# One order for r's sums at every place below slot 896, and no product at place 12

## What is computed

```
mixed = tanh(x @ W_in.T + b_in + cond)
h1 = GRU(mixed); h2 = GRU(h1)            # 1024 steps each, one after another
   # step: r = sigmoid(xr + hr); z = sigmoid(xz + hz)
   #       n = tanh(xn + r * hn); h = (1 - z) * n + z * h
gate = sigmoid(cond @ W_gate.T + b_gate)
x = x + (gate * h2 + h2) @ W_out.T + b_out
shared = silu(x @ w1) * (x @ w3) @ w2                      # HS = 512
s = sigmoid(concat(x, cond) @ router_W); top 2 of 8 by s + router_bias
routed = sum over the chosen experts of weight * gelu(x @ W1e) @ W2e
out = x + (shared + routed) / 3
```

## Time and profile before

| | |
|---|---|
| time, median of 3 runs | 2154.06 us (2152.3 to 2155.34) |
| the profiled execution: time | 2159.05 us |
| its span, first to last instruction | 2157.3 us |
| its granted TensorE clock | 0.999 |
| PE, DVE, ACT, POOL busy | 95%, 84%, 52%, 26% of the span |
| instructions | 162,384, of them 70,040 matmuls and 70,040 weight loads |

### The profile page before, as it was taken

One profiled execution on the slowest core, in us unless ns is written; L12 is line 12 of the kernel. 1 busy time (PEld: TensorE's weight loads), 2 busy tenths in 40 slices (PEclk: granted clock), 3 DMA queues, 4 the chain that ended last, 5 costly groups with the idle time before them and its releaser, 6 DMA issues.

```text
span 2157.3 us, 162384 instructions
## 1 busy us (share of the span) xinstructions
PE 2057.2 (95%) x70040; PEld 1503.5 (70%) x70040; DVE 1818.3 (84%) x11337; ACT 1128.8 (52%) x6471; POOL 563.1 (26%) x2540
## 2 busy tenths in 40 slices
PE   6999999999999999999999999999999999999997
PEld 4666667777677776777667777677767777777776
DVE  3888888888888888888888888898888888888885
ACT  2555555555555555555555555555555555555542
POOL 1222232222322223222232222322232222222220
PEclk9999999999999999999999999999999999999999
DMA  5000000000000000000000000000000000000000
GB/s 222 5 5 5 4 5 5 5 5 5 10 5 5 5 5 10 5 5 5 10 5 5 5 5 10 5 5 5 5 10 5 5 5 10 5 5 9 5 5 9
DMA packets 7184, 24.32 MB, mean 11 GB/s; under 512 B 1584, under 2 KB 3904, under 8 KB 6208
## 3 DMA queue, kind: packets, MB, share of 16 engines
q1 hardware_dynamic: 6464, 13.93, 1.7%
HBM read 11.83 MB, written 2.10 MB: 6 GB/s over the span
## 4 chain that ended last, share of the span: by engine, by line
PE 72%; DVE 18%; ACT 7%; issue 2%; DMA 0%; SPq 0%; DVEq 0%
PE bank L336 34%; PE bank L328 20%; PE bank L268 14%; DVE bank L407 6%; DVE cells L427 5%; ACT factors L489 4%; DVE z_pre L408 3%; PE bank L309 3%; DVE r_pre L398 3%; ACT cells L493 2%; DVE bank L416 0%; PE bank L275 0%; DMA x_t<-in_x_t 0%; DVE n_second L383 0%; DVE x L707 0%
## 5 line engine op out<-in xcount | busy, mean ns | idle before, releaser
L336 PE MATMUL bank<-w_h,cells 128*22 128x128 f32 (+4 forms) x32768 | 1379.0, 281 | 20.3 <-DVE cells L427 11.8
L336 PEld LDWEIGHTS bank<-w_h,cells 128*22 128x22 f32 (+4 forms) x32768 | 867.5, 111 | 128.3 <-DVE cells L427 82.1
L328 PEld LDWEIGHTS bank<-w_h,cells 128*2 128x2 f32 (+15 forms) x28112 | 527.8, 113 | 480.4 <-DVE cells L427 452.2
L534 POOL TENSOR_SCALAR cells<-cells 128x4 f32<-128x4 f32 x2048 | 466.7, 228 | 1498.8 <-DVE cells L427 1497.9
L328 PE MATMUL bank<-w_h,cells 128*2 128x64 f32 (+15 forms) x28112 | 784.0, 225 | 65.5 <-DVE cells L427 53.6
L483 ACT ACTIVATE n_second<-r_pre 128x4 f32<-128x4 f32 x2048 | 426.4, 208 | 517.9 <-DVE r_pre L398 475.5
L489 ACT ACTIVATE factors<-z_pre 128x4 f32<-128x4 f32 x2048 | 429.4, 210 | 475.2 <-DVE z_pre L408 428.8
L427 DVE TENSOR_TENSOR_SCAN cells<-factors,cells 128x18 f32<-128x18 f32 x2048 | 396.5, 194 | 215.8 <-ACT cells L493 140.6
L407 DVE STREAM_TRANSPOSE bank<-bank 128x64 f32<-128x64 f32 x2048 | 522.4, 255 | 57.3 <-PE bank L336 34.8
L398 DVE STREAM_TRANSPOSE r_pre<-bank 128x64 f32<-128x64 f32 x2048 | 483.8, 236 | 33.3 <-PE bank L328 21.9
L408 DVE STREAM_TRANSPOSE z_pre<-bank 128x64 f32<-128x64 f32 x2048 | 428.9, 209 | 0.0
(11 more groups left out here) (93 smaller groups left out, 616.4 us busy)
## 6 DMA issues: line engine op xcount, KB each, us to landing
x_t<-in_x_t SPq DMA_DIRECT2D x4, 512.0 KB, 6.8
w_1e<-in_w_1e SPq DMA_DIRECT2D x1, 2048.0 KB
w_2e<-in_w_2e SPq DMA_DIRECT2D x1, 2048.0 KB
w_x<-in_w_x SPq DMA_DIRECT2D x2, 768.0 KB, 8.0
w_h<-in_w_h SPq DMA_DIRECT2D x2, 768.0 KB, 9.4
w<-in_w SPq DMA_DIRECT2D x3, 512.0 KB
out_y<-y SPq DMA_DIRECT2D x6, 256.0 KB, 3.3
w_in<-in_w_in SPq DMA_DIRECT2D x1, 256.0 KB, 2.7
```

The costliest lines, as they stand in the source:

```text
L328: mm = pe.matmul(r_sums[l][p][32 * g:32 * g + B * (j + 1)], state_tile(l, j, kt), w_h[l][:, kt, g, 2 * U:], start=False, stop=False, tile_ ...
L336: mm = pe.matmul(sums[l][p][32 * g:32 * g + B * (j + 1), 0:width], state_tile(l, j, kt), w_h[l][:, kt, g, 0:width], start=False, stop=Fals ...
L534: pool.tensor_scalar(cell_part(step_rows(l, j), 3), cell_part(step_rows(l, j), 1), 0.5, None, ALU.mult)\
```

## The change

Below slot 896 `r_first` is true at all places; from 896 on it is false at 0, 4, 8 and 12 as before. In windows of 128 steps PE may have no mixture product at place 12; the planner then puts the same products into later half slots.

```
 def r_first(l, t):
     s = t + LAG * l
-    return s % CH not in ((0, 4, 8, 12) if s >= SHORT else (4, 12))
+    return s < SHORT or s % CH not in (0, 4, 8, 12)
...
     def busy(self, engine, h):
         j, part = (h // 2 + self.begin) % CH, h % 2
         if engine == "pe":
-            return j in projection_pieces(part ^ 1) or part == 1 and (self.sparse or self.window > 5 * CH and j % 8 != 6)
+            return j in projection_pieces(part ^ 1) or part == 1 and (self.sparse or self.window > 5 * CH and j % 8 != 6) or self.sparse and j == 12
```

## The result

The changed kernel takes 2213.1 us in the median (2208.66 to 2218.07, 5 runs) against 2155.34 us for the kernel before (2152.3 to 2160.56, 5 runs): the ratio is 1.0276, 95% interval 1.0247 to 1.0304. It is slower by 2.8%, 58 us. I had forecast slower by 0.5%, 2165.7 us, with 2185 as the upper end. The direction was right; the size was not, and the time lies outside the range, above my "stop after stop" rival of 2201 us.

A forecast was written before the change was run, and what follows sets the result against it. Bound by the dependency chain, with instruction supply close under it: +14.1 us in slots 152 to 895, −3.4 plus 0.9 put back in 19 to 151, total +11.6, so 2165.7 us median; range 2143 to 2185.

The forecast's parts named there:

- stop after stop: Rival: with no slack left, supply stops lock one after another; 3.705 us per block, 2201 us; chance 0.13.
- What bounds the kernel: Dependency chain of the two layers, with PE's instruction supply, blocks of 127.6 weight loads, as a second bound close under it.
- 84 with a stop: Slots 160 to 783, kernel before: of 214 blocks touching no one-bank slot, 84 counted as having a stop.
- Order of r: Places 4 and 12 below slot 896: r's transpose precedes the other layer's scan; 0.2 us less, if PE keeps up.
- priced 12 as ordinary: Place 12 without product: PE's work of 1.71 us fits the slot, so −0.20 us.
- Instructions: 3,552 more weight loads and matmuls each, 548 to 576 blocks; slots 160 to 783: 352.0 x 3.62 = 1274.2 us, +11.8.
- Every block is of the sort that took 3.62 us: Slots 160 to 783: one-bank slots' slack gone, every block takes the 3.62 us mean of blocks touching none.
- The correction that I made downward: Per-block time taken as 3.62 us, not the 3.64 seen in runs, since blocks would hold 3.46 against 3.50 us of path.
- Hidden: Rival: supply is hidden or waits no more often than now; only the path counts, −16 us, 2138 us; chance 0.22.
- It cancels: Rival: blocks of 3.585 us give no change in slots 160 to 783; 2152 to 2156 us; chance 0.15.
- The new wait is on DVE: Rival: r's early transpose blocks DVE, delaying layer 1's scan at place 4; path gives −12 rather than −16 us; no chance given.
- the signs that I had named: 576 packets, some 31,660 L328 loads, issue waits of 40 to 60 us, one-bank scan gap 0.83, mean slot about 2.04.

The follow-up runs named there:

- run with wide products: Changed kernel with each mixture product made by one matmul over the whole array in place of four over strips of 32; 2263.49 us, ratio 1.0473.
- before, one strip: Kernel before with only the first of the four strips of each mixture product, except in the last group; 2118.55 us, ratio 0.9783.
- four from slot 152: Kernel before with one-bank steps at places 0, 4, 8 and 12 from slot 152 on, at 4 and 12 before that; 2138.97 us, ratio 0.9934.
- four in all slots: Kernel before with one-bank steps at places 0, 4, 8 and 12 in all slots; 2151.03 us, ratio 0.9936.
- three: Kernel before with one more one-bank place below slot 896, 8 beside 4 and 12; 2155.87 us, ratio 0.995.
- changed, one strip: Changed kernel with only the first of the four strips of each mixture product, except in the last group; 2146.3 us, ratio 0.9914 to the kernel before.
- products alone: Kernel before with no product at place 12 in groups of 128 steps, order of r unchanged; 2160.3 us, ratio 1.0032.
- place 4 alone: Kernel before with the new order of r only at place 4; place 12 stays one-bank and keeps its product; 2182.64 us, ratio 1.0138.
- place 12 alone: Kernel before with the new order of r and no product only at place 12; place 4 stays one-bank below slot 896; 2187.21 us, ratio 1.0109.
- order alone: Kernel before with the new order of r at all places below slot 896, products still allowed at place 12; 2223.69 us, ratio 1.0285.
- before with padding: Kernel before with eight one-column matmuls into a spare PSUM column behind each one-bank step below slot 896; 2230.11 us, ratio 1.0316.
- before, flooded: Kernel before with eight more one-column matmuls of zero weights in each step of layer 0 below slot 896; 2506.97 us, ratio 1.1641.
- experiments 1 and 5: Kernel before with tiny matmuls added: behind each one-bank step (1; 2230.11 us), or in every layer 0 step (5; 2506.97 us), both below slot 896.

## Why the prediction was right in kind and wrong in size

The stretch of slots 160 to 783 in one profiled execution of each run, ordered by its weight loads. The run with wide products is left out, since its products hold PE longer.

| kernel | weight loads | blocks (/ 127.6) | us | us per block |
|---|---|---|---|---|
| before, one strip | 39,780 | 311.8 | 1233.9 | 3.96 |
| four from slot 152 | 39,920 | 312.9 | 1248.2 | 3.99 |
| four in all slots | 39,920 | 312.9 | 1248.8 | 3.99 |
| three | 41,173 | 322.7 | 1258.2 | 3.90 |
| changed, one strip | 42,277 | 331.3 | 1253.2 | 3.78 |
| products alone | 42,405 | 332.3 | 1261.4 | 3.80 |
| before | 42,422 | 332.5 | 1262.4 | 3.80 |
| place 4 alone | 43,668 | 342.2 | 1279.0 | 3.74 |
| place 12 alone | 43,672 | 342.3 | 1294.1 | 3.78 |
| changed | 44,914 | 352.0 | 1311.6 | 3.73 |
| order alone | 44,916 | 352.0 | 1316.6 | 3.74 |
| before with padding | 44,914 | 352.0 | 1319.5 | 3.75 |
| before, flooded | 52,415 | 410.8 | 1516.8 | 3.69 |

At some 312 blocks the path sets the time (the waits for issue are 1.3 us in the second row); from 340 on the time per block stays near 3.7, and the time goes mostly by the count; the kernel before lies between, where both bounds count.

**What bounds the kernel: right.** That stops come a multiple of some 128 loads apart, that the two bounds lie close together, and that the second is the supply of instructions holds in every run that bears on it. In the prediction, "84 with a stop" of the dense blocks is more than the 72 waits of the whole stretch in the table, which leaves out the shortest; counted down to 0.1 us, the same trace has 88.

**Order of r: right for the slot, wrong for its neighbour.** The 0.2 us were won at places 4 and 12. I had a cost for place 4 only, where a product stands beside the projection, and priced 12 as ordinary. In fact the projection alone makes PE late with the first step behind it, and the slots at places 5 and 13 take 0.14 us more. The term was −0.27 us for 16 slots and −0.40 in the early slots; where no stop falls it measured −0.14 and −0.23. The early stretch so won less than I had credited it, and stops came there (3.5 us of waits, 0.4 us before): +1.9 us in this execution, and between −1.3 and +0.5 in the three others of the same early program.

**Instructions: the count right, the time per block mis-sized. This is the step that failed.** "Every block is of the sort that took 3.62 us": the 214 dense blocks of the kernel before were not of one sort. They are a mixture of blocks that PE's path set, shorter, and of blocks that the supply set; those behind a one-bank slot came at 3.58. The change shifts the mixture: 172 waits in 352 blocks, where the kernel before had 72 in 332. Blocks behind a stop had taken 3.705 in the trace of before, and it is this figure, which I had put into the rival, that came near: the changed kernel has 3.726. The nearness is in part luck, since only half of its blocks end with a stop. 352.0 x (3.726 − 3.62) = 37.3 us of the 45.1 us between the 2170.7 that I forecast for a profiled execution and the 2215.85 that it took; slots 784 to 895 add 3.4 us for the same reason (+5.5 where I had 7 x 0.30 = 2.1), and slots 32 to 143 4 us. The correction that I made downward, because a block after the change holds less path time, works only for blocks that the path sets; in one that ends with a stop, less path time only makes the stop longer, as the landings in the last section have it.

Of the signs that I had named, the 576 packets and the 31,664 loads of L328 came; the waits for issue went past the 40 to 60 us, and the mean slot to 2.10 us instead of 2.04.

**The rule of the Trainium skill.** The Trainium skill (Runtime: NRT & Kernel Launch, Instruction fetch mechanics) has blocks of 256 instructions, which agrees with 576 packets for 2 x 73,592 records, and has the crossing of a block mostly hidden. Here that holds for 40,000 loads in 624 slots (1.3 us of waits) and fails for 45,000 (72.0 us of waits).

**Rivals.** "Hidden" is out (experiments 1 and 5). "It cancels" is out by the result. "The new wait is on DVE": PE's lateness behind a projection is there, at 0.14 us, and changed a size, as said. "Stop after stop" came nearest with its 2201 us, and should have had the larger chance: in slots 160 to 783 the kernel before has no stop at places 12 and 13 and one at place 5, and the change takes this slack away. Its mechanism, one stop bringing the next until they lock, is only half there. Cut at the starts of the packets of PE's instruction queue, a block with a stop is followed by another in 59% of cases, one without in 38%; before, it was 33% and 19%.

What stays open is the cause of the 0.3% that the restriction on products costs alone: its profiled execution took 2157.67 us and that of the kernel before 2159.05, so this pair can't show it.

## What to carry to other kernels

A fully unrolled program of short instructions can have a second bound, as this one has: how fast the engine gets its instructions. Look for "issue" waits in the middle of runs of equal instructions, count the instructions between them, and price every edit in instructions as well as in microseconds of the path; here 32 weight loads and 32 matmuls were a quarter of a block, 0.93 us where the supply is the bound, and bought 0.2 us of path, of which 0.14 were given back in the next slot. When an edit takes away the slack that a second bound lives on, take that bound's own pace from where it binds (behind a stop), not a mean over a mixture.

## What the runs showed of the hardware

- When flooded, PE took 256 instructions (128 weight loads, 128 matmuls) in 3.69 us in the mean, 14.4 ns for each. In 331 blocks of the flooded run that both began and ended with a stop, the packet of 16 KB started 1.26 us after PE went on with the block before, took 1.08 us, and PE went on 1.39 us after it had landed, together 3.73 us. The stops of the other kernels end in the same way: 1.42 us after a landing in the median of the changed kernel's 227 (1.27 to 1.52 for the middle 80%), 1.39 in the kernel before. That ties the stops to the packets without any change of the program. PE thus seems to hold one block in advance and no more; that is read from the order of these events and was not tested by itself.
- The pace of the supply varies: half of these 331 periods lie between 3.48 and 3.88 us, with a median of 3.745.
- For float32, four matmuls side by side in strips of 32 output rows hold the array for 0.44 us for 128 x 256 outputs; one matmul of 128 rows holds it for 0.63 us and starts 0.11 us later behind the group before it.
